# One-hot tiles of the source counts: a column read with a stride of nought in place of a per-partition scalar

## The reference

```python
def gat_conv(x, src, dst, W, att_src, att_dst, bias, heads, C, concat):
    h = (x @ W).reshape(n, heads, C)
    ...
    e = jax.nn.leaky_relu(a_src[src] + a_dst[dst], NEG_SLOPE)
    emax = jax.ops.segment_max(e, dst, num_segments=n)
    ex = jnp.exp(e - emax[dst])
    denom = jax.ops.segment_sum(ex, dst, num_segments=n)
    alpha = ex / (denom[dst] + 1e-16)
    out = jax.ops.segment_sum(h[src] * alpha[:, :, None], dst, num_segments=n)
```

## Time and profile before

| what | us |
|---|---|
| median of 3 runs | 6756.64 |
| lowest and highest | 6749.88 and 6773.88 |
| span of the profiled execution | 7555.6 |

### The profile page before, as it was taken

One profiled execution on the slowest core, in us unless ns is written; L12 is line 12 of the kernel. 1 busy time (PEld: TensorE's weight loads), 2 busy tenths in 40 slices (PEclk: granted clock), 3 DMA queues, 4 the chain that ended last, 5 costly groups with the idle time before them and its releaser, 6 DMA issues. The chain is left out here.

```text
span 7555.6 us, 86623 instructions
## 1 busy us (share of the span) xinstructions
PE 4855.1 (64%) x23532; PEld 3254.8 (43%) x23532; DVE 4654.8 (62%) x13695; ACT 3050.2 (40%) x6979; POOL 3999.0 (53%) x3991
## 2 busy tenths in 40 slices
PE   6888888779978625686233443434899995579211
PEld 4666665445558403575222222211555553346111
DVE  4777666223358627668674455656899995644444
ACT  3555554443334103344343333333677773245000
POOL 4565553544435466556555565656333334654766
PEclk9999999889989755796555666766899997789555
DMA  6988665776768423696343475754677675565232
GB/s 143 226 240 231 209 206 188 215 215 226 243 201 245 121 45 92 187 257 185 109 122 103 124 118 110 128 96 88 234 248 256 244 251 156 173 183 177 84 88 73
DMA packets 1104141, 1292.14 MB, mean 171 GB/s; under 512 B 133903, under 2 KB 815679, under 8 KB 1097390
## 3 DMA queue, kind: packets, MB, share of 16 engines
q1 hardware_dynamic: 973518, 1032.63, 43.5%
q0 software_dynamic: 130144, 253.97, 16.5%
HBM read 607.93 MB, written 682.10 MB: 171 GB/s over the span
## 5 line engine op out<-in xcount | busy, mean ns | idle before, releaser
L570 POOL DMA_INDIRECT jk_layer_msg<-jk,idx_jk x588 | 593.7, 1010 | 376.5 <-issue 173.4
L1057 PE MATMUL jk_layer_sum_ps<-ident,jk_layer_weighted 128*128 128x128 f32 x784 | 178.9, 369 | 733.6 <-ACT jk_layer_weighted L1023 382.1
L2084 POOL TENSOR_TENSOR rows_moved<-rows_x_in,w_lonely_row 128x512 f32<-128x512 f32 x98 | 124.6, 1272 | 677.3 <-DVE rows_x L671 640.9
L1057 PEld LDWEIGHTS jk_layer_sum_ps<-ident,jk_layer_weighted 128*128 128x128 f32 x784 | 114.6, 183 | 844.8 <-ACT jk_layer_weighted L1023 431.5
L1079 DVE TENSOR_TENSOR_SCAN jk_layer_sum_t<-goes_on,jk_layer_sum_t,jk_layer_sum_ps 128x512 f32<-128x512 uint8 x196 | 250.1, 1276 | 346.3 <-DMA sage_nodes_x_in<-in_x 288.0
L1886 ACT ACTIVATE jk_layer_h_t<-jk_layer_h_ps,w_jk_b 128x512 f32<-128x512 f32 x196 | 134.7, 687 | 631.8 <-DMA gat_own<-yv 337.9
L696 PE MATMUL sage_nodes_h_ps<-sage_nodes_h_t,w_ws 128*128 128x512 f32 x784 | 353.6, 594 | 0.0
L1198 DVE COPY sage_h<-sage_turn 128x512 f32<-128x512 f32 x98 | 67.8, 692 | 456.7 <-PE sage_turn L687 348.3
L894 ACT ACTIVATE sage_nodes_h_t<-sage_nodes_h_ps,w_b_c 128x512 f32<-128x512 f32 x392 | 248.9, 688 | 239.8 <-PE sage_nodes_h_ps L696 114.8
L696 PE MATMUL sage_h_ps<-sage_sum_t,w_wn 128*128 128x512 f32 x588 | 296.7, 614 | 59.0 <-issue 58.8
L2283 PE MATMUL gcn_end_sum_ps<-ident,gcn_end_rows 128*128 128x128 f32 x196 | 54.7, 434 | 426.9 <-DVE gcn_end_rows L2276 215.4
(11 more groups left out here) (454 smaller groups left out, 16299.8 us busy)
## 6 DMA issues: line engine op xcount, KB each, us to landing
h<-sage_nodes_h SPq DMA_DIRECT2D x196, 512.0 KB
h_t<-sage_h_t SPq DMA_DIRECT2D x98, 512.0 KB
h<-sage_h SPq DMA_DIRECT2D x98, 512.0 KB
jk_t<-jk_layer_h_t SPq DMA_DIRECT2D x196, 256.0 KB
rows_layers<-jk_t SPq DMA_DIRECT2D x49, 1024.0 KB, 5.9
r<-rows_h SPq DMA_DIRECT2D x98, 512.0 KB
second_x_in<-u SPq DMA_DIRECT2D x147, 260.0 KB
jk<-jk_layer_h SPq DMA_DIRECT2D x147, 256.0 KB
```

The source lines that it names most:

```text
L570: pool.indirect_dma_start(out=into[:, g.number % depth, s, :], out_offset=None, in_=table, in_offset=bass.IndirectOffsetOnAxis(ap=index_ti ...
L1057: mm = pe.transpose(ps[:, c, at_s], self.weighted[:, g.b, s, c * P:(c + 1) * P], self.K.ident[:])
L2084: pool.tensor_tensor(moved[:, g.b], x_in[:, g.number % 3], to_subs(W.lonely_row), ALU.add).then_inc(lonely_added.sem, 1)
```

## The change

Both comparisons become an operation on two tensors. The second is the same column, read with a stride of nought, so that each partition's float appears 512 or 128 times. The values written are the same; the tiles, the semaphores, the buffers and the order of the instructions stay, and so does the number of instructions.

```diff
     def vector_hot(self, dve, t):
         wait_for(dve, self.hot_used, Group(t - 2))
-        dve.tensor_scalar(self.lo_hot[:, t % 2, :], self.K.lo_iota[:], self.K.src_lo[:, t:t + 1], None, ALU.is_equal)
-        dve.tensor_scalar(self.hi_hot[:, t % 2, :], self.K.hi_iota[:], self.K.src_hi[:, t:t + 1], None, ALU.is_equal).then_inc(self.hot_ready.sem, 1)
+        dve.tensor_tensor(self.lo_hot[:, t % 2, :], self.K.lo_iota[:], self.K.src_lo[:, t:t + 1].broadcast_to([P, GROUP]), ALU.is_equal)
+        dve.tensor_tensor(self.hi_hot[:, t % 2, :], self.K.hi_iota[:], self.K.src_hi[:, t:t + 1].broadcast_to([P, P]), ALU.is_equal).then_inc(self.hot_ready.sem, 1)
```

## The result

The changed kernel takes 6791.2 us (median of 8 runs, 6785.3 to 6800.1), the kernel before 6771.85 us (median of 8 runs). The ratio is **1.0037, 95% interval 1.0024 to 1.0049**: slower by about 25 us (0.0037 × 6771.85; the interval is 16 to 33 us), where 26.5 were forecast. The two medians alone differ by 19.4 us and the two means by 24.7, so the times give the size only roughly; the stage in the traces gives it more sharply. The profiled execution of the kernel before that stands ahead of the prediction was 12% longer than its timed runs, and its slow middle is not found again (experiment 1), so the profile after is read against the stage as the prediction had worked it out, and against a second profile of the kernel before.

A forecast was written before the change was run, and what follows sets the result against it. The gather on GpSimd was taken to bound the stage, 254.8 us before and 281.3 after: +26.5 us (98 × 0.27). Added to 6756.6 this gave 6783 us, range 6744 to 6806.

The forecast's parts named there:

- slow middle: Count chain in the first profile: 89 columns at 2.7 us each, taken as waits absent from timed runs.
- The gather sets the stage's end: Stage before the change: GpSimd's gather ends after 254.8 us, the count chain on VectorE and TensorE after 132.3 us.
- The rate: VectorE comparisons: `lo` paced at 0.61 us because its second input is float, `hi` at 0.20, a column 0.81 us.
- Hidden cover: Count chain grows from 132.3 to 158.8 us, but costs nothing by itself under the gather's 254.8 us.
- The hold-up and the lock: GpSimd DMAs wait for VectorE operations with two SBUF inputs, locking at 1.62 us per two columns: +26.5 us; chance 0.57.
- One reading on the way: In another stage, operations beside the DMAs read PSUM for one input, and no DMA lasts over 0.962 us.
- the gather isn't held up more: Rival: DMAs beside the chain take 1.35 or even 1.25 us, up to 9.8 us less, 6747 to 6757 us; chance 0.18.
- The chain as the bound: Rival: the count chain ends the stage in timed runs too, costing 18 us, 6775 us; chance 0.12.
- the faster case: Rival: the early pace causes the slow stretch, which a slower column avoids: −28 us, 6729 us; chance 0.05.
- The slow stride: Rival: stride of nought makes `lo` 1.28 us, a column about 1.5: +40 to +75, about 6815 us; chance 0.08.
- The price of the present form: Today's DMAs beside the chain last 1.05 instead of 0.95 us: 98 × 0.10 = 9.8 us.
- The weak step: A GpSimd DMA waits only for the rest of the current `lo`, 0.37 us, then is let go at its end.

The follow-up runs named there:

- experiment 1: The kernel before, unchanged, run once more for a second profile: 6733.27 us, beside a median of 6745.83 for the runs of the kernel before.
- experiment 2: The changed kernel with both columns first copied to PSUM, so each comparison has one SBUF and one PSUM input: ratio 0.9988 to the kernel before.

## Why the prediction was right

- **The gather sets the stage's end.** Right, and shown: chain 132.6, gather 254.3 us in the second profile of before (132.3 and 254.8 worked out).
- **The rate.** `lo` 0.695 us, `hi` 0.293, a column 0.80 us (0.81 taken). The reason given, the float input, was half of it: the stride of nought alone gives the same 693 ns.
- **Hidden cover.** The chain grew by 26 us to 158.4, and that cost nothing by itself: with PSUM columns it is as long and the kernel isn't slower.
- **The hold-up and the lock.** Right, and shown: 1.30 us a DMA, 1.60 apart, 98 of them; 25.0 us for the stage against 26.5, most of the difference being the column, 196 × (0.804 − 0.675) = 25.3. That the second input in SBUF is the cause is shown by experiment 2, where the same operations with that input in PSUM cost nothing. One reading on the way was too wide: beside the DMAs of the earlier trace rows not every operation reads PSUM (the batch-norm statistics at L1688 read one SBUF tensor); what holds is that none has two SBUF inputs.
- **The time itself.** That 6791.2 us came so near to 6783 is in part luck. The forecast started from 6756.64, the median of three runs, and over eight runs the kernel before took 6771.85; what the prediction can be held to is the difference.
- **The rivals.** That the gather isn't held up more falls with the 1.30 us. The chain as the bound, and the faster case built on it, fall with the second profile of before. The slow stride falls with 695 ns. The price of the present form, 9.8 us, was real: with either input in PSUM the gather falls from 254.3 to 244.5 and 244.3 us.
- **The weak step.** That a DMA waits only for the rest of the operation under way is true of the changed kernel, where 97 of 98 did, and it isn't a rule. With one operation more to the column that rule put the gather at 252 to 258 us, where 392.7 and 413.5 were measured.

## What to carry to other kernels

Where GpSimd issues indirect DMAs and sets the pace, an operation on VectorE costs first by what it reads beside them: here a comparison of 743 ns that reads PSUM was cheaper than one of 352 ns on SBUF. Where it reads only SBUF, its length counts through the period in which the two lock: 695 ns on two SBUF tensors (two columns in 1.61 us) cost 25 us, and 425 ns (two columns in 1.27 us, beside a DMA's own 1.25) cost nothing. To tell such a price, look for the same DMA in the trace with and without the neighbour (0.95, 1.05, 1.30 us), and see in what period the two lock. A row of operations on two SBUF tensors without a break is best kept away from a gather: with two to a column it cost 25 us, with three 138 to 159 (gathers of 392.7 and 413.5 beside 254.3); one operation in between that reads PSUM bounded each wait at 0.5 us.

## What the runs showed of the hardware that I had not expected

A single indirect DMA on GpSimd was stuck for 147.75, 170.11 and 170.12 us while VectorE ran operations on two SBUF tensors without a gap, three to a column, and went on when the last of them was through. What lets it through or keeps it out stays open. The section "SBUF: two separate sides" of "SBUF — State Buffer" in the Trainium skill says that the loser blocks for the whole instruction of the other; the waits in the changed kernel agree (0.35 us, the rest of one `lo`), these don't: they outlast some 505 to 580 operations (168 and 195 columns of 0.87 us, three to a column).

And the pace of the kernel with `hi` alone changed fell in with the gather's by itself: 1.26 us for two columns beside 1.25 for a DMA, with hardly a wait left, on the same count of instructions.
